# One exponent instruction per key tile in a two-layer gated cross-attention kernel

## What is computed

```python
def _L1_xattn_ref(query, key, value, mask, wq_kernel, ...):
    q = split_heads(query @ wq_kernel + wq_bias)
    k = split_heads(key @ wk_kernel + wk_bias)
    v = split_heads(value @ wv_kernel + wv_bias)
    scores = jnp.einsum('bhqd,bhkd->bhqk', q, k) / jnp.sqrt(jnp.float32(HD))
    scores = jnp.where(mask[:, None] == 0, -1e9, scores)
    attn = jax.nn.softmax(scores, axis=-1)
    out = jnp.einsum('bhqk,bhkd->bhqd', attn, v)
    return out.transpose(0, 2, 1, 3).reshape(b, -1, D) @ wo_kernel + wo_bias

x = x + tanh(g_xattn[0]) * _L0_xattn_ref(_layernorm(x), ctx, ctx, ...)
x = x + tanh(g_ffn[0])   * _L0_ffn_ref(_layernorm(x), ...)
x = x + tanh(g_xattn[1]) * _L1_xattn_ref(_layernorm(x), ctx, ctx, mask, ...)
x = x + tanh(g_ffn[1])   * _L1_ffn_ref(_layernorm(x), ...)
```

## Time and profile before

| what | value |
|---|---|
| runs (three) | 957.93, 967.49, 972.21 us; median 967.49 us |
| the profiled execution | 965.04 us, of which the span from the first to the last instruction is 963.2 us |
| busy share of the span | PE 89%, DVE 72%, ACT 61%, POOL 56% |
| exponent instructions | 768, of 542 ns each |
| granted TensorE clock | 0.971 of full speed on the mean |

### The profile page before, as it was taken

How to read it: one execution, slowest core, us unless ns; L and a number is a source line. 1 busy time by engine, 2 the same in 40 slices (tenths; PEclk the granted TensorE clock), 3 DMA queues, 4 the chain that set the end, 5 groups by cost and what they waited for, 6 DMA issues and landing times.

```text
span 963.2 us, 33056 instructions
## 1 busy us (share of the span) xinstructions
PE 861.1 (89%) x13273; PEld 620.4 (64%) x13273; DVE 697.7 (72%) x1545; ACT 591.7 (61%) x1085; POOL 538.8 (56%) x733
## 2 busy tenths in 40 slices
PE   3898899898899988989999999998999999999975
PEld 1365667676666766767667666666766666666754
DVE  4778777858778686776757858787777868687724
ACT  2267576565755757666575576757676666757570
POOL 5647754546456364654556557676675667672202
PEclk9989999999999999999999999999999999999995
DMA  5344543212222222223667747687776766675300
GB/s 149 96 131 127 164 120 98 90 47 77 79 81 88 62 66 71 87 76 94 125 113 148 145 86 149 136 170 141 154 146 134 160 123 152 122 143 108 59 2 19
DMA packets 103555, 104.48 MB, mean 108 GB/s; under 512 B 28442, under 2 KB 97388, under 8 KB 103404
## 3 DMA queue, kind: packets, MB, share of 16 engines
q1 hardware_dynamic: 101792, 102.03, 45.6%
q10 hardware_dynamic: 1612, 0.36, 0.2%
HBM read 35.89 MB, written 0.46 MB: 38 GB/s over the span
## 4 chain that ended last, share of the span: by engine, by line
PE 56%; DVE 20%; ACT 11%; issue 6%; POOL 3%; ACTq 1%; DMA 1%; SPq 0%; POOLq 0%; DVEq 0%
PE pO L1295 12%; PE pST L1274 11%; DVE mx L1153 10%; PE pMX L1316 9%; PE pKV L1361 5%; PE pKV L1352 5%; ACT P L856 3%; PE pF L1425 3%; PE pF L1461 3%; ACT HR L865 2%; ACT L856 2%; DVE HR L1033 1%; ACT V L888 1%; DVE rden L1078 1%; ACT L865 1%
## 5 line engine op out<-in xcount | busy, mean ns | idle before, releaser
L1153 DVE TENSOR_REDUCE mx<-pMX 112x1 f32<-112x500 f32 x768 | 490.3, 668 | 101.7 <-PE pMX L1316 97.3
L856 ACT ACTIVATE P<-pST 125x448 f32<-125x448 f32 x768 | 389.5, 542 | 226.6 <-PE pST L1274 222.7
L1316 PE MATMUL pMX<-kop,qmax 48*112 48x500 f16 (+1 forms) x768 | 277.2, 403 | 12.0 <-DMA qmax<-qlo 6.9
L1274 PE MATMUL pST<-qexp,kop 50*128 50x112 f16 (+2 forms) x3072 | 268.2, 215 | 19.8 <-ACT P L856 16.6
L1274 PEld LDWEIGHTS pST<-qexp,kop 50*128 50x128 f16 (+2 forms) x3072 | 182.8, 100 | 99.1 <-ACT P L856 42.6
L1295 PE MATMUL pO<-P,V 125*18 125x112 f32 x6144 | 189.4, 265 | 4.5 <-issue 4.4
L1295 PEld LDWEIGHTS pO<-P,V 125*18 125x18 f32 x6144 | 139.2, 99 | 39.1 <-issue 19.8
L665 POOL CAST khi<-kfull 128x500 f16<-128x500 f32 x96 | 57.6, 600 | 140.9 <-ACT kfull L883 140.5
L1316 PEld LDWEIGHTS pMX<-kop,qmax 48*112 48x112 f16 (+1 forms) x768 | 97.7, 131 | 57.2 <-DVE mx L1153 20.1
L667 POOL TENSOR_TENSOR klo<-kfull,khi 128x500 f16<-128x500 f32 x96 | 109.1, 1136 | 7.8
L794 POOL TENSOR_TENSOR Clo<-C,Chi 128x500 f16<-128x500 f32 x93 | 105.7, 1136 | 7.5
(11 more groups left out here) (170 smaller groups left out, 1195.9 us busy)
## 6 DMA issues: line engine op xcount, KB each, us to landing
C<-in_ctxT SPq DMA_DIRECT2D x31, 750.0 KB, 7.4
kop<-maskop SPq DMA_DIRECT2D x48, 437.5 KB
kop<-khi SPq DMA_DIRECT2D x192, 62.5 KB
kop<-khi SPq DMA_DIRECT2D x96, 125.0 KB
kop<-klo SPq DMA_DIRECT2D x96, 62.5 KB
kop<-klo SPq DMA_DIRECT2D x48, 125.0 KB
maskin<-in_mask SPq DMA_DIRECT2D x8, 656.2 KB, 4.9
qexp<-qmax SPq DMA_DIRECT2D x16, 182.0 KB
```

Of the source, the lines that this page charges most:

```text
L856: nc.scalar.activation(P[0:KP, slot, h * 4 * T:(h + 1) * 4 * T], pST[0:KP, h, 0:4 * T], ACT.Exp, scale=EXP_SCALE).then_inc(exp_done, 1)
L1153: nc.vector.tensor_reduce(mx[:, s % 2, c, p:p + 1], pMX[0:T, m % 3, 0:CW], AX.X, ALU.max).then_inc(max_done, 1)
L1274: mm = nc.tensor.matmul(pST[0:keys.stop - keys.start, h, i * T:(i + 1) * T], kop[rows, b, slot, keys], qexp[rows, b, slot, :, :].rearrange ...
L1316: nc.tensor.matmul(pMX[0:T, m % 3, 0:CW], qmax[rows, b, slot, :, :].rearrange("r j q -> r (j q)"), kop[rows, b, slot, c * CW:(c + 1) * CW] ...
```

## The change

The two exponent instructions of a tile become one, of 125 x 896 elements, which reads both banks of pST (the tile's two halves, 448 of 512 columns in each) and writes the tile's whole slot of P. It waits for both halves' scores. `exp_done` now counts tiles and not halves; so half 0 of a tile's scores waits for the whole exponent of the previous tile, half 1 has no wait of its own, and `weigh` waits once per tile. On ACT, the evacuation of a slot of the second layer, which stood between the two exponents, now stands before the one.

```diff
--- before.py
+++ after.py
@@ -845,15 +845,15 @@
                     act.wait_ge(bc_in, 16)
                     nc.scalar.activation(gains[:, :], bc[:, GX:GX + 4], ACT.Tanh).then_inc(init_a, 1)
 
-            def exps(st, kt, h):
+            def exps(st, kt):
                 back, tile = tile_at(kt, E_LAG)
                 if not is_batch(st.s - back):
                     return
                 slot = tile % RING
-                act.wait_ge(st_ready, st.at(lambda s: 2 * (KT * (s - back) + tile) + h + 1))
-                if h == 0 and (st.s > back or tile >= RING):
+                act.wait_ge(st_ready, st.at(lambda s: 2 * (KT * (s - back) + tile) + 2))
+                if st.s > back or tile >= RING:
                     act.wait_ge(av_done, st.at(lambda s: KT * (s - back) + tile - RING + 1))
-                nc.scalar.activation(P[0:KP, slot, h * 4 * T:(h + 1) * 4 * T], pST[0:KP, h, 0:4 * T], ACT.Exp,
+                nc.scalar.activation(P[0:KP, slot, :].rearrange("k (h n) -> k h n", h=2), pST[0:KP, :, 0:4 * T], ACT.Exp,
                                      scale=EXP_SCALE).then_inc(exp_done, 1)
 
             def gelus(s):
@@ -894,10 +894,9 @@
                     if has_f(s) and kt == 10:
                         evacuate(kt)
                     early_loads(s, kt)
-                    exps(st, kt, 0)
                     if not side_by_side and not (has_f(s) and kt == 10):
                         evacuate(kt)
-                    exps(st, kt, 1)
+                    exps(st, kt)
                     if side_by_side and not (has_f(s) and kt == 10):
                         evacuate(kt)
                     if s in (2, 3) and kt in (1, 3, 5, 7):
@@ -1264,8 +1263,8 @@
                 if h == 0:
                     score_operands(n, tile)
                 b, keys = n % 2, keys_of(tile)
-                if n > 0 or tile > 0:
-                    pe.wait_ge(exp_done, 2 * (KT * n + tile) + h - 1)
+                if h == 0 and (n > 0 or tile > 0):
+                    pe.wait_ge(exp_done, KT * n + tile)
                 for i in range(HP):
                     if layer_of(n) == 0:
                         rows, slot = slice(HALF * h, HALF * h + ROWS_L0), i
@@ -1288,8 +1287,8 @@
                     if st.s > back:
                         pe.wait_ge(o_free, st.at(lambda s: s - back))
                 for tile in (last - 1, last):
+                    pe.wait_ge(exp_done, KT * (st.s - back) + tile + 1)
                     for r in range(2):
-                        pe.wait_ge(exp_done, 2 * (KT * (st.s - back) + tile) + r + 1)
                         for g in range(4):
                             p = 4 * r + g
                             mm = nc.tensor.matmul(pO[32 * g:32 * g + VW, r * T:(r + 1) * T],
```

## The result

The changed kernel takes 1087.64 us (median of four runs, 1082.4 to 1091.34); the kernel before, in the runs beside it, 965.84 us. The ratio is 1.125, with a 95% interval of 1.121 to 1.129: slower by 122 us. The prediction was 1057 with a range of 1025 to 1095: the right side and inside the range, but 31 us short.

What follows compares the result with a forecast made beforehand. The prediction took PE's one queue to bound both layers. It added 66 us (second layer) and 23 us (first) to 965.0 for 1054, then 2.5 us for the median: 1057 us, range 1025 to 1095.

Steps and rivals of the forecast that it cites:

- PE's queue bounds, ACT's time is worth nothing: Both layers run at PE's pace; ACT's saving of some 30 us falls in free time and counts as nothing.
- The exponent's length: On ACT, the merged exponent of 896 elements takes 0.90 us, bounded by 0.88 and 1.08.
- Rival D: Merged exponent on ACT costs two full lengths, 1.08 us: 29 us more, 1086 in all; chance 0.12.
- The second layer's stand: PE stands 0.83 us in six gaps a batch, 80 us; 66 left after covered gaps and vanished waits.
- the 4.1 us that were taken off as a wait for DVE: Second layer: the weighted sums' wait on PE after DVE empties pO, 4.1 us, was expected to go.
- The first layer's stand: PE stands about 0.5 us in four gaps a batch after odd slots, 32 us; 23 left after vanished waits.
- the hand-over to ACT: First layer: ACT starts the exponent 0.14 us after the scores' end.
- the waits of PE that went away: First layer, taken off: 3.7 us of waits for half 1's exponents and 5.4 for DVE emptying pF.
- rival A: PE's short stands make the granted clock fall in 28 batches, 1.5 us each: 42 us more, 1099; chance 0.10.
- against it: the batches at 1.00 have idle gaps too: Argument against added clock falls: full-clock batches already have PE idle for a tenth of their length.
- the named band: Second layer: batches should grow by 2.5 to 6.5 us, else the predicted sizes are wrong.
- PE's waits for P from 59 to 120 to 160 us: Sign: PE's waits for exponents before pST's matmuls grow from 59 to 120 to 160 us; under 80 refutes.

Runs made afterwards that it cites:

- both layers filled: Changed kernel plus repeated, unneeded maximum products on PE where it would stand, in the first and second layer; 1070.45 us, ratio 1.109.
- the run that filled the second alone: Changed kernel plus three repeated, unneeded maximum products on PE before the exponent wait in the second layer's odd slots; 1053.53 us, ratio 1.092.
- the filled kernel before: Kernel before the change plus two unneeded maximum products on PE ahead of the experts' output products in each even step; 963.01 us, ratio 0.9968.

## Why the prediction was right, and what was short

- **PE's queue bounds, ACT's time is worth nothing.** Right: ACT's busy time fell by 34 us and the kernel is 122 us slower.
- **The exponent's length,** 0.90 us by a row of another function and memory: 0.916 measured. Rival D, two full lengths, is out. The Trainium skill's formula (ScalarE: Activation LUTs, "What ACT_TABLE_LOAD costs") gave 932 ns; the measured length lies between this and the 903 ns from the rows.
- **The second layer's stand,** 66 us: right. Without falls the layer takes 479.8 us with the change (both layers filled; 481.1 in the run that filled the second alone, with one fall of some 1.3 us) and 418.8 without it (the filled kernel before): 61 us. One term of it was misread: the 4.1 us that were taken off as a wait for DVE stand in the earlier trace rows as "issue", with no engine named.
- **The first layer's stand,** 23 us: somewhat too large. The layer is 27.7 us longer, 8 of them by the clock (next point), so some 19 are left: 0.8 and 1.1 us in most of its batches at full clock, about 3 in its first and its last. The terms that were mis-sized are the hand-over to ACT, 0.07 us and not 0.14 at the gap shown, and the waits of PE that went away: half 1 follows half 0 sooner now, so the weighted sums behind the gap of the earlier trace rows begin only 0.32 us later (1.55 us after the scores' end, 1.23 before) and not 0.40.
- **The clock** was the failure. The prediction had it as rival A, 42 us with a chance of 0.10, beside a forecast in which nothing was added for it. In the second layer it costs 517.5 - 481.1 = 36 us, some 6 of which the kernel before paid too; in the first, three batches at 35.3 us where their like take 32.5, 8 us. Without the clock the sum would have been too high by some 9 us (66 and 23 against 61 and 19); with it, it is 31 us short. So A's 42 us came nearly whole, but in another way: not 28 batches at 1.5 us each, but 14 at some 3. That the time still lies in the range is in part luck: the range's upper end was set by D, which did not happen, and by a part of A, and a stand put too high made up for some of the clock. The step that failed is "against it: the batches at 1.00 have idle gaps too": one batch's idle time at full clock says nothing on how much more is free of charge. With a stand of 4 us in each batch the four falls of the second layer became falls in 11 of its 16 batches.
- **What would show it:** the clock's mean is 0.93, under the 0.95 that was named for A. The batches of the second layer at full clock grew by 4.0 us, in the named band. "PE's waits for P from 59 to 120 to 160 us" was a wrong measure: the 59 was the sum of PE's row and its weight loads' row, which wait in the same gap (0.75 and 1.08 us in the one before 676.67); the sum went to 245. PE's row alone, 16.6 to 102.7, grew by 86 us.

## What to carry to other kernels

Two PSUM banks with one reader instruction each are a double buffer; one instruction over both is a single buffer, and the producer stands for up to the reader's whole length wherever its own queue has nothing long between. So look for each such gap in the producer's order, and merge only there where it is covered; where the reader is not the bound, as here, even that gained nothing (972.9 us against 965.0). A stand of PE can cost twice, by itself and by the granted clock, and not only where the clock already fell: batches 3, 7 and 11 of the first layer had no fall before and have one now. Price the fall (a batch with, a batch without) and put it into the sum, not beside it. If the stand can't be removed, matmuls that nobody needs kept the clock here (0.90 to 1.00 in the second layer), as long as they were fewer than the gap holds.

## What was not expected

- Half a microsecond decides over much more: one uncovered gap of 0.4 us in eight batches of the first layer took its clock from 0.99 to 0.94 and cost 17 us (989.8 against 972.9).
- The same stands don't give the same falls: 30.3 us for batch 20 in two kernels, the odd batches some 0.6 us apart, and clocks of 0.90 and 0.97 over the layer. What tips it between them is open.
- Falls come in pairs: in the changed kernel's second layer a fall of 3.4 us is followed four times, 6.8 us after its begin, by one of 13.7 us or more. Whether the first brings the second isn't shown.
